# Quantising rows inside the product that follows, turned by transposing DMAs, and a ring of eight residual tiles in the last stage

## The chip, the cores and the metric

The kernel runs on one core of a Trainium2 chip. The metric is the device time in microseconds of one execution, the median of several runs. TensorE (PE) multiplies, ScalarE (ACT) evaluates functions, VectorE (DVE) and GpSimd (POOL) work elementwise, and SyncE (SP) and POOL issue the DMAs named below.

## The reference, cut to what matters

Two gated blocks, each attention and a feed-forward layer, run over x of 16 x 256 rows of 512 float32. The change touches the end of the second one only:

```python
h = _layernorm(x, ln_g, ln_b)
h = _qlinear(h, w1)                       # (4096 x 512) by (512 x 2048)
h = jax.nn.gelu(h, approximate=False)
out = _qlinear(h, w2)                     # (4096 x 2048) by (2048 x 512)
x = x + jnp.tanh(g_ffn[1]) * out

def _quant_act_int8(x):
    amax = jnp.maximum(jnp.quantile(jnp.abs(x), 1.0 - 0.005), EPS)
    s = 127 / amax
    q = jnp.clip(jnp.round(x * s), -128, 127) / s
```

`_qlinear` quantises its input by one scale for the whole tensor (`_quant_act_int8`) and its weights to -1, 0 and 1. The scale needs a quantile over all elements, so each of the two layers has to wait for a search.

## The kernel before, in words

The 4096 rows are 32 tiles of 128 rows (`TILES`), in 8 batches (`NB`) of 4 tiles (`WB`). The program is a row of stages. Each is a block with a list for each engine and semaphores of its own, and ends in two barriers of all engines with the clearing of the semaphores between them (L113 is the barrier), so work of one stage doesn't overlap that of the next. The stages that matter:

- `quantile1` (to L1833) finds `amax1`, the first scale, and puts the ternary first weights into `w1T`.
- `quantise_hidden` (L1836): for each of 8 batches DVE rounds (L1864) and clips (L1866) `hid`, 128 x 2048 float32, in place. ACT converts it to bf16 integers `q` (L1878), TensorE transposes its 16 blocks of 128x128 into PSUM (L1895), and ACT and DVE each copy a half to `qT` (L1881, L1869). An identity for TensorE is loaded by SP first (L1850), and DVE begins with a cast of it (L1856), then `full` and `scale` (L1857, L1859). TensorE runs a batch behind DVE and ACT.
- `product_tops` (L1919): 32 groups of products (L1904), 28 wide ones (2 tiles, half of the 2048 columns) and 4 narrow ones (1 tile, all columns). Two PSUM halves `bz` take turns. ACT applies gelu (L1961, L1959) into `Gs`, three buffers of four tiles: two lie in the memory of `hid`, which is free by then, the third is its own. SP spills each tile, 1 MB, to `g_d` (the tensor `activations`, L1934), and DVE takes maxima of every tile into `cand` (L1975). From the fourth batch on ACT waits until the batch that lay in its buffer is spilled and its maxima are taken.
- `quantile2` finds the second scale from `cand` and makes `w2T`.
- `ffn` (L2186), run once as `p8_`: SP reloads the spilled tiles (L2235) into 13 slots, the last three batches being resident. ACT counts (L2283) and rounds every second tile (L2285), DVE rounds the others (L2315), clips all into a ring of four `Gq` (L2320), TensorE multiplies (L2267), and DVE adds the residual (L2339). `output(n)` runs on DVE `LAG` = 3 tiles behind. The residual comes by POOL's queue in batches of 4 tiles, 1 MB, into two buffers `y` (L2246), and the sums are stored from them (L2252). A new batch can be loaded when the store of the one that lay in the buffer has landed. The last batch is stored by SP, tile by tile (L2238).
- `quantile2_of_all` and a second `ffn` (`p9_`) are run only if a flag says that the search over the maxima wasn't enough.

The order on each queue is the order of the code. `groups` and `ready` are tables written out before the run: group i belongs to tiles n, n + 1, and `ready[n]` is the number of gelus after which tile n is complete.

## Time and profile before

| | |
|---|---|
| time, median of 3 runs (lowest, highest) | 1515.62 us (1513.62, 1519.42) |
| the profiled execution | 1515.95 us |
| its span on the core | 1514.1 us |
| busy: PE, DVE, ACT, POOL | 1237.0, 996.2, 733.6, 352.3 us |
| bytes moved by DMA | 261.85 MB, 173 GB/s in the mean |

The rows that the prediction uses stand further below, in numbered groups. In a timeline each row has the start of an instruction or of a merged run of them in us from the start of the span, its length, the engine (SPq is a DMA issue on SP), the line, the operation with output and inputs, the count, and in brackets the idle time of the engine just before it, with what ended it. Buffer names are the program's, with the number left out and prefixes cut to p_ or q_; `residual` is the DRAM tensor that POOL loads `y` from. A stretch row gives busy time by engine and, behind it, the clock that TensorE was granted (1.00 is full) and the mean busy share of the 16 DMA engines.

### The profile page before, as it was taken

The page shows a single profiled execution, that of the slowest core. Times are in us where ns is not written, and L with a number is a line of the kernel's source. Part 1 is how long each engine was busy: PE and PEld are TensorE (multiplying, and loading weights), DVE is VectorE, ACT ScalarE, POOL GpSimd, SP SyncE. Part 2 cuts the span into 40 slices and gives each one's busy share as a digit, 9 for nine tenths or more (in the row PEclk, how much of TensorE's full clock was granted, in tenths as well). Part 3 has the DMA queues.
Part 4 walks back from the last instruction along what each step waited for, and adds up shares of the span by engine and source line. Part 5 has one row for each costly group of instructions (what it writes and reads, how often), then busy time and mean ns, then how long its engine had stood idle before and what let it go on. Part 6 is the DMA issues. An engine that isn't in the chain of part 4 may idle for free. (4 is left out here: it accounts for less than half of the span.)

```text
span 1514.1 us, 25958 instructions
## 1 busy us (share of the span) xinstructions
PE 1237.0 (82%) x9458; PEld 922.0 (61%) x9458; DVE 996.2 (66%) x2309; ACT 733.6 (48%) x1129; POOL 352.3 (23%) x339
## 2 busy tenths in 40 slices
PE   6899999999999846999993999992424999246986
PEld 5788888888888735766651566651313888242433
DVE  5677777767766633444432599994776699676573
ACT  3233333333343321456442466663835555677990
POOL 1233333333343230111000167663000000000120
PEclk9999999999999967999997999995555999556998
DMA  6032122221222119689668999933000577215973
GB/s 220 22 112 71 72 77 90 96 85 70 74 72 101 47 57 372 214 292 317 231 241 323 380 330 329 345 121 127 18 1 3 227 310 325 87 56 214 399 275 113
DMA packets 89723, 261.85 MB, mean 173 GB/s; under 512 B 9585, under 2 KB 21009, under 8 KB 81425
## 3 DMA queue, kind: packets, MB, share of 16 engines
q1 hardware_dynamic: 78976, 226.81, 40.1%
q0 software_dynamic: 7664, 32.51, 6.3%
q10 hardware_dynamic: 2976, 1.14, 0.3%
q8 instruction: 63, 1.03, 0.3%
q14 instruction: 44, 0.35, 0.1%
HBM read 155.32 MB, written 105.12 MB: 172 GB/s over the span
## 5 line engine op out<-in xcount | busy, mean ns | idle before, releaser
L921 PEld LDWEIGHTS p_sel<-p_pick,p_xp 128*128 128x128 bf16 x1536 | 89.3, 100 | 59.0 <-issue 34.1
L921 PE MATMUL p_sel<-p_pick,p_xp 128*128 128x128 bf16 x1536 | 100.6, 224 | 25.4 <-DMA p_xp<-xparts 22.4
L1904 PE MATMUL p_z<-qT,w1T 128*128 128x256 bf16 (+1 forms) x1152 | 113.9, 263 | 2.1 <-PEq L113 2.1
L1059 DVE COPY p_selT<-p_sel 128x512 f32<-128x512 f32 x64 | 44.3, 692 | 104.2 <-PE p_sel L921 104.2
L1904 PEld LDWEIGHTS p_z<-qT,w1T 128*128 128x128 bf16 x1152 | 102.6, 98 | 13.4 <-issue 2.4
L2246 POOL DMA_DIRECT2D p_y<-residual x8 | 8.4, 1053 | 392.6 <-POOLq L113 335.3
L2267 PE MATMUL p_o<-w2T,p_Gq 128*128 128x512 bf16 x384 | 88.4, 392 | 11.5 <-DVE p_Gq L2320 11.5
L1975 DVE MAX8 cand<-hid 128x8 f32<-128x128 f32 x384 | 75.1, 277 | 16.9 <-ACT hid L1961 16.9
L1004 ACT ACTIVATE p_selT<-p_sel 128x512 f32<-128x512 f32 x64 | 38.2, 597 | 91.1 <-PE p_sel L921 91.1
L341 PE MATMUL p_M<-p_ctxTh,p_Wkh 128*128 128x256 f32 x256 | 76.0, 297 | 1.9 <-DVE p_Wkl L667 1.9
L341 PE MATMUL p_M<-p_xnTh,p_Wqh 128*128 128x256 f32 x256 | 75.0, 293 | 0.8 <-DVE p_V L740 0.8
L2267 PEld LDWEIGHTS p_o<-w2T,p_Gq 128*128 128x128 bf16 x384 | 38.3, 101 | 60.5 <-DVE p_Gq L2320 13.0
L341 PE MATMUL p_M<-p_ctxTh,p_Wkl 128*128 128x256 f32 x256 | 73.1, 286 | 0.0
L341 PE MATMUL p_M<-p_ctxTl,p_Wkh 128*128 128x256 f32 x256 | 73.0, 285 | 0.0
L341 PE MATMUL p_M<-p_xnTh,p_Wql 128*128 128x256 f32 x256 | 72.1, 282 | 0.0
L341 PE MATMUL p_M<-p_xnTl,p_Wqh 128*128 128x256 f32 x256 | 72.0, 281 | 0.0
L511 ACT ACTIVATE p_qT<-p_M,p_bqT 128x256 f32<-128x256 f32 x64 | 26.8, 470 | 84.0 <-PE p_M L341 84.0
L1253 PE MATMUL p_O<-p_cin,p_eT 128*128 128x512 f32 x128 | 62.9, 619 | 2.2 <-ACT p_eT L1321 2.2
L1728 PE MATMUL q_tot<-q_cnt,q_ones 128*128 128x4 f32 x32 | 9.2, 359 | 65.4 <-DVE q_junk L1778 33.0
L1235 PE MATMUL p_S<-p_ctxT,p_xnT 128*128 128x256 f32 x256 | 61.1, 382 | 0.2 <-ACT p_xnT L1307 0.2
L962 PE MATMUL p_lay<-p_f,p_inner 64*128 64x512 f32 x208 | 58.5, 639 | 2.8 <-DVE p_stage L1051 2.8
L601 POOL TENSOR_TENSOR p_xb<-p_xin,p_tgbo 128x1024 f32<-128x1024 f32 x16 | 39.0, 2439 | 91.2 <-DVE p_sharedk L791 75.0
(320 smaller groups left out, 3519.1 us busy)
## 6 DMA issues: line engine op xcount, KB each, us to landing
inter_d<-p_stage SPq DMA_DIRECT2D x64, 512.0 KB, 4.3
p_rows<-inter_d SPq DMA_DIRECT2D x32, 1024.0 KB, 9.0
activations<-hid SPq DMA_DIRECT2D x24, 1024.0 KB, 6.0
p_cin<-in_ctx_dram SPq DMA_DIRECT2D x32, 512.0 KB, 5.2
xparts<-p_parts SPq DMA_DIRECT2D x16, 768.0 KB, 3.2
hid<-activations SPq DMA_DIRECT2D x10, 1024.0 KB, 10.2
p_xp<-xparts SPq DMA_DIRECT2D x3, 3072.0 KB, 25.1
p_xin<-in_x_dram SPq DMA_DIRECT2D x16, 512.0 KB, 4.1
```

Of the source, the lines that this page charges most:

```text
L341: mm = pe.matmul(out, left[a][:, c, lcols], right[e][:, c, rcols], start=(k == 0), stop=(k == len(terms) - 1))
L511: a = act.activation(dst[:, c, :], bM[k][:, (c % 2) * S:(c % 2 + 1) * S], ACT.Identity, bias=bias[:, c:c + 1])
L601: pool.tensor_tensor(xb[par][:, :, :], xin[par][:, :, :], tgbo[:, :].rearrange("p (a d) -> p a d", a=1).broadcast_to([P, NT, D]), ALU.add) ...
L921: mm = pe.matmul(bsel[u % 2][:, k * P:(k + 1) * P], xp[:, c, tile, r, :], pick[sb % 2][:, tile, :, :].rearrange("p s g -> p (s g)"), start ...
L962: mm = pe.matmul(bank(n, a)[:, :], inner[rows, j, h * P:(h + 1) * P], f2s[i // PAIRS][rows, j % (PAIRS // 2), :], start=True, stop=True)
L1004: act.activation(*picked(q, u), ACT.Copy).then_inc(s["sel_act"], 1)
L1059: dve.tensor_copy(*picked(q, u)).then_inc(s["sel_dve"], 1)
L1235: mm = pe.matmul(bS[:, t * S:(t + 1) * S], xnT[:, c, t * P:(t + 1) * P], ctxT[b % 2][:, c, :], start=(c == 0), stop=(c == C - 1))
L1253: mm = pe.matmul(bO[t][:, :], eT[:, k, t, :], cin[b % CD][:, k, :], start=(k == 0), stop=(k == NT - 1))
L1904: mm = pe.matmul(bank, w1T[:, c, fc * P:(fc + 1) * P], qT[:, c, bass.ds(first, n)], start=(c == 0), stop=(c == C - 1))
L1975: a = dve.max(cand[:, c:c + 8], Gs[j % R][:, t, :, k * OCT:(k + 1) * OCT])
L2267: mm = pe.matmul(bo[n % len(bo)][:, :], Gq[n % QR][:, k, :], w2T[:, k, :], start=(k == 0), stop=(k == FC - 1))
```

## The change

`quantise_hidden` goes. Its work moves into `product_tops`, in pairs of tiles (`NPAIR` = 16):

- DVE computes `full` and `scale`, then rounds and clips all 16 pairs of `hid` one after the other, with the product's own scale `zs` after the second; its maxima come behind them.
- ACT converts pairs 0 to 4 at once and the other eleven after the first eight gelus (2, 1, 1, 2, 1, 1, 2, 1 of them), into a ring of four bf16 buffers `q`.
- SP issues one transposing DMA for each pair (128 x 1024 bf16, 256 KB, on-chip memory to on-chip memory), nine before the first spill and the others among the spills. TensorE waits for the pair's DMA at each group.
- `qT` is now laid out by tile, [P, TILES, C, P], so a product over two tiles reads two runs of 128 columns. No identity, no transposes on TensorE, no copies out of PSUM. One stage with its barriers less.
- `Gs` changes its order: the buffer outside `hid` comes first, and ACT waits at the second and third batch until the pairs that lie there are converted.

In `ffn` the two `y` buffers of four tiles become eight of one tile (`YR`), each with its semaphores. POOL loads and stores tiles of 256 KB: a store after each tile, and behind it a load into the buffer whose store was issued `BEHIND` = 2 tiles before, once that has landed. `LAG` is 4.

```diff
-def quantise_hidden(nc, hid, K, amax, scale, qT):
...
 PAIR = 2 * P
 HALF = FC // 2
 NARROW = WB
+NPAIR = TILES // 2
+
+
+def z_product(pe, bank, w1T, qT, fc, first, tiles):
+
+    for c in range(C):
+        mm = pe.matmul(bank, w1T[:, c, fc * P:(fc + 1) * P], qT[:, bass.ds(first, tiles), c, :], start=(c == 0), stop=(c == C - 1))
+    return mm
 
 
...
 
-def product_tops(nc, qT, w1T, gam, amax, zs, Gs, g_d, cand):
+def product_tops(nc, hid, qT, w1T, gam, amax, zs, Gs, g_d, cand):
 
     groups = product_groups()
     ready = [max(i for i, (first, tiles, *_) in enumerate(groups) if first <= n < first + tiles) + 1 for n in range(NB * WB)]
+    QB, EARLY = 4, 5
+    late = list(range(EARLY, NPAIR))
+    after_gelu = {g: [late.pop(0) for _ in range(k)] for g, k in enumerate((2, 1, 1, 2, 1, 1, 2, 1))}
+    assert not late
     with ExitStack() as es:
         bz = [es.enter_context(nc.psum_tensor(f"p7_z{i}", [P, FC * P], F32)) for i in range(2)]
-        s = es.enter_context(semaphores(nc, "p7_", ["scale_own", "scale_done", "z_full", "gelu_done", "max_done"] + [f"spilled{i}" for i in range(len(Gs))]))
+        q = [es.enter_context(nc.sbuf_tensor(f"p7_q{i}", [P, 2, D], BF16)) for i in range(QB)]
+        full, scale = [es.enter_context(nc.sbuf_tensor("p7_" + n, [P, 1], F32)) for n in ("full", "scale")]
+        s = es.enter_context(semaphores(nc, "p7_", ["own", "scale_done", "rounded", "clipped", "q_done", "z_full", "gelu_done", "max_done"]
+                                        + [f"turned{i}" for i in range(QB)] + [f"spilled{i}" for i in range(len(Gs))]))
         block = es.enter_context(nc.Block())
         R = len(Gs)
+        pair = lambda k: hid[:, 2 * k:2 * k + 2, :]
 
         @block.sync
         def _(sp):
+
+            def turn(k):
+                sp.wait_ge(s["q_done"], k + 1)
+                sp.dma_start_transpose(qT[:, 2 * k:2 * k + 2, :, :].rearrange("p t c n -> p (t c) n"), q[k % QB][:, :, :].rearrange("p t d -> p (t d)")).then_inc(s[f"turned{k % QB}"], 16)
+
+            turns = 0
             for n in range(NB * WB):
+                while turns < min(NPAIR, 9 + 3 * (n // 2)):
+                    turn(turns)
+                    turns += 1
                 j, t = divmod(n, WB)
                 sp.wait_ge(s["gelu_done"], ready[n])
                 sp.dma_start(g_d[:, j, t], Gs[j % R][:, t]).then_inc(s[f"spilled{j % R}"], 16)
@@ -1938,15 +1891,26 @@
         @block.tensor
         def _(pe):
             for i, (n, tiles, f0, nf) in enumerate(groups):
+                k = n // 2
+                pe.wait_ge(s[f"turned{k % QB}"], 16 * (k // QB + 1))
                 if i >= 2:
                     pe.wait_ge(s["gelu_done"], i - 1)
                 bank = bz[i % 2][:, :].rearrange("p (f n) -> p f n", f=nf)
                 for f in range(nf):
-                    mm = z_product(pe, bank[:, f, :], w1T, qT, f0 + f, n * P, tiles * P)
+                    mm = z_product(pe, bank[:, f, :], w1T, qT, f0 + f, n, tiles)
                 mm.then_inc(s["z_full"], 1)
 
         @block.scalar
         def _(act):
+
+            def integers(k):
+                act.wait_ge(s["clipped"], k + 1)
+                if k >= QB:
+                    act.wait_ge(s[f"turned{k % QB}"], 16 * (k // QB))
+                act.activation(q[k % QB][:, :, :], pair(k), ACT.Copy, bias=-MAGIC).then_inc(s["q_done"], 1)
+
+            for k in range(EARLY):
+                integers(k)
             act.wait_ge(s["scale_done"], 1)
             for i, (n, tiles, f0, nf) in enumerate(groups):
                 j, t = divmod(n, WB)
@@ -1954,19 +1918,36 @@
                     if t == 0 and f0 == 0:
                         act.wait_ge(s[f"spilled{j % R}"], 16 * WB * (j // R))
                     act.wait_ge(s["max_done"], n - R * WB + tiles)
+                elif j and t == 0 and f0 == 0:
+                    act.wait_ge(s["q_done"], j * NPAIR // 2)
                 act.wait_ge(s["z_full"], i + 1)
                 if tiles == 1:
                     act.activation(Gs[j % R][:, t], bz[i % 2][:, :].rearrange("p (f n) -> p f n", f=nf), ACT.Gelu, scale=zs[:, 0:1]).then_inc(s["gelu_done"], 1)
                 else:
                     act.activation(Gs[j % R][:, t:t + tiles, f0:f0 + nf, :], bz[i % 2][:, :].rearrange("p (f t n) -> p t f n", f=nf, t=tiles),
                                    ACT.Gelu, scale=zs[:, 0:1]).then_inc(s["gelu_done"], 1)
+                for k in after_gelu.get(i, ()):
+                    integers(k)
 
         @block.vector
         def _(dve):
-
-            dve.tensor_scalar(zs[:, 0:1], amax[:, 0:1], 1.0 / QMAX, None, ALU.mult).then_inc(s["scale_own"], 1)
-            dve.wait_ge(s["scale_own"], 1)
-            dve.tensor_tensor(zs[:, 0:1], zs[:, 0:1], gam[:, 0:1], ALU.mult).then_inc(s["scale_done"], 1)
+            n_ = Count(dve)
+
+            def own():
+                dve.wait_ge(s["own"], n_.next(s["own"]))
+
+            dve.reciprocal(full[:, :], amax[:, 0:1]).then_inc(s["own"], 1)
+            own()
+            dve.tensor_scalar(scale[:, :], full[:, :], QMAX, None, ALU.mult).then_inc(s["own"], 1)
+            own()
+            for k in range(NPAIR):
+                dve.tensor_scalar(pair(k), pair(k), scale[:, :], MAGIC, ALU.mult, ALU.add).then_inc(s["rounded"], 1)
+                dve.wait_ge(s["rounded"], k + 1)
+                dve.tensor_scalar(pair(k), pair(k), MAGIC + QMAX, MAGIC + QMIN, ALU.min, ALU.max).then_inc(s["clipped"], 1)
+                if k == 1:
+                    dve.tensor_scalar(zs[:, 0:1], amax[:, 0:1], 1.0 / QMAX, None, ALU.mult).then_inc(s["own"], 1)
+                    own()
+                    dve.tensor_tensor(zs[:, 0:1], zs[:, 0:1], gam[:, 0:1], ALU.mult).then_inc(s["scale_done"], 1)
             for n in range(NB * WB):
                 j, t = divmod(n, WB)
                 dve.wait_ge(s["gelu_done"], ready[n])
...
-    R, QR, LAG = len(Gs), 4, 3
+    R, QR, LAG, YR, BEHIND = len(Gs), 4, 4, 8, 2
...
-        y = [sbt(f"y{i}", [P, WB, D]) for i in range(2)]
+        y = [sbt(f"y{i}", [P, D]) for i in range(YR)]
...
-                for t in range(WB):
-                    sp.wait_ge(s["y_done"], WB * (NB - 1) + t + 1)
-                    sp.dma_start(ov[:, order[NB - 1] * WB + t, :], y[(NB - 1) % 2][:, t, :]).then_inc(s["y_last"], 16)
+                for n in range(NB * WB - WB, NB * WB):
+                    sp.wait_ge(s["y_done"], n + 1)
+                    sp.dma_start(ov[:, token_tile(n), :], y[n % YR][:, :]).then_inc(s["y_last"], 16)
                 sp.wait_ge(s["y_last"], 16 * WB)
 
         @block.gpsimd
         def _(pool):
             with when(pool, flag):
 
-                def load_x(i):
-                    pool.dma_start(y[i % 2][:, :, :], x3_d[:, order[i] * WB:(order[i] + 1) * WB, :]).then_inc(s[f"x_in{i % 2}"], 16)
-
-                load_x(0)
-                load_x(1)
-                for i in range(NB - 1):
-                    pool.wait_ge(s["y_done"], WB * (i + 1))
-                    pool.dma_start(ov[:, order[i] * WB:(order[i] + 1) * WB, :], y[i % 2][:, :, :]).then_inc(s[f"y_out{i % 2}"], 16)
-                    if i + 2 < NB:
-                        pool.wait_ge(s[f"y_out{i % 2}"], 16 * (i // 2 + 1))
-                        load_x(i + 2)
-                for par in range(2):
-                    pool.wait_ge(s[f"y_out{par}"], 16 * len(range(par, NB - 1, 2)))
+                def load_x(n):
+                    pool.dma_start(y[n % YR][:, :], x3_d[:, token_tile(n), :]).then_inc(s[f"x_in{n % YR}"], 16)
+
+                for n in range(YR):
+                    load_x(n)
+                for n in range(NB * WB - WB):
+                    pool.wait_ge(s["y_done"], n + 1)
+                    pool.dma_start(ov[:, token_tile(n), :], y[n % YR][:, :]).then_inc(s[f"y_out{n % YR}"], 16)
+                    m = n - BEHIND
+                    if m >= 0 and m + YR < NB * WB:
+                        pool.wait_ge(s[f"y_out{m % YR}"], 16 * (m // YR + 1))
+                        load_x(m + YR)
+                for k in range(YR):
+                    pool.wait_ge(s[f"y_out{k}"], 16 * len(range(k, NB * WB - WB, YR)))
 
...
                 def output(n):
-                    i, t = divmod(n, WB)
+                    here = y[n % YR][:, :]
                     dve.wait_ge(s["o_used"], n + 1)
-                    if t == 0:
-                        dve.wait_ge(s[f"x_in{i % 2}"], 16 * (i // 2 + 1))
-                    dve.scalar_tensor_tensor(y[i % 2][:, t, :], bo[n % len(bo)][:, :], coef[:, :], y[i % 2][:, t, :], ALU.mult, ALU.add).then_inc(s["y_done"], 1)
+                    dve.wait_ge(s[f"x_in{n % YR}"], 16 * (n // YR + 1))
+                    dve.scalar_tensor_tensor(here, bo[n % len(bo)][:, :], coef[:, :], here, ALU.mult, ALU.add).then_inc(s["y_done"], 1)
 
...
-    Gs = [room[:, k * FC:(k + 1) * FC, :].rearrange("p (t a) (b n) -> p t (a b) n", t=WB, b=WB) for k in range(2)] + [sbt("third", [P, WB, FC, P])]
+    Gs = [sbt("third", [P, WB, FC, P])] + [room[:, k * FC:(k + 1) * FC, :].rearrange("p (t a) (b n) -> p t (a b) n", t=WB, b=WB) for k in range(2)]
...
-        qT = sbt("qT", [P, C, TILES * P], BF16)
-        quantise_hidden(nc, hid, K, amax1, scale, qT)
+        qT = sbt("qT", [P, TILES, C, P], BF16)
```

## Rows read from the trace of the kernel before

**Rows 1.** The page: the span, and the queue of the small constants.

```profile
span 1514.1 us, 25958 instructions
...
q10 hardware_dynamic: 2976, 1.14, 0.3%
```

**Rows 2.** Stretches: length, busy us (count) of PE, PEld, DVE, ACT, POOL, clock, DMA share, GB/s.

```profile
1131.00:1171.40 40.40, 14.69 (x128) 12.63 (x129) 25.48 (x28) 22.69 (x16) 0.00 (x0) 0.54 0.01 3
...
1182.00:1291.70 109.70, 103.28 (x1072) 93.88 (x1069) 100.22 (x512) 59.10 (x31) 0.00 (x0) 0.99 0.75 307
...
1412.00:1424.00 12.00, 12.00 (x57) 5.49 (x56) 3.69 (x4) 11.81 (x11) 2.03 (x2) 1.00 1.01 422
```

**Rows 3.** Timeline (start, us, engine): the quantising stage and the product's start.

```profile
1136.13 0.33 SPq L1850 DMA_DIRECT2D p_ident<-in_c_ident_dram  x1
1137.98 0.23 DVE L1856 CAST p_identb<-p_ident 128x128 bf16<-128x128 f32 x1 [6.86 <-DMA p_ident<-in_c_ident_dram]
...
1138.51 1.29 DVE L1864 TENSOR_SCALAR hid<-hid,scale 128x2048 f32<-128x2048 f32 x1
...
1140.97 1.28 DVE L1864 TENSOR_SCALAR hid<-hid,scale 128x2048 f32<-128x2048 f32 x1
...
1167.39 1.89 PE L1895 MATMUL p_t<-p_identb,p_q 128*128 128x128 bf16 x16 [1.53 <-ACT p_q L1878]
...
1171.42 11.79 PE L1904 MATMUL p_z<-qT,w1T 128*128 128x256 bf16 x92 [2.14 <-PEq L113]
```

**Rows 4.** Timeline of ACT and DVE in the product, beginning and end.

```profile
1176.67 1.28 ACT L1961 ACT_TABLE_LOAD   x1 [6.33 <-PE p_z L1904]
...
1182.11 6.28 DVE L1975 MAX8 cand<-hid 128x8 f32<-128x128 f32 x32 [10.34 <-ACT hid L1961]
...
1183.69 1.97 ACT L1961 ACTIVATE hid<-p_z,zs 128x2048 f32<-128x2048 f32 x1 [1.61 <-PE p_z L1904]
1187.18 1.97 ACT L1961 ACTIVATE hid<-p_z,zs 128x2048 f32<-128x2048 f32 x1 [1.53 <-PE p_z L1904]
...
1285.37 1.97 ACT L1959 ACTIVATE hid<-p_z,zs 128x2048 f32<-128x2048 f32 x1 [1.61 <-PE p_z L1904]
```

**Rows 5.** Timeline of ACT and DVE in the search before: operations on 128x1024.

```profile
1119.34 1.06 ACT L1712 ACTIVATE q_junk_a<-q_over 128x1024 bf16<-128x1024 f32 x1
...
1124.14 0.75 DVE L1765 TENSOR_SCALAR q_junk<-cand,q_cur 128x1024 f32<-128x1024 f32 x1
```

**Rows 6.** DMA issues: out<-in, queue, count, KB each, median us to landing.

```profile
p_vrep<-global_values SPq DMA_DIRECT2D x16, 256.0 KB, 3.5
...
out_dram<-p_y SPq DMA_DIRECT2D x4, 256.0 KB, 2.0
```

**Rows 7.** Timeline of PE in the last stage.

```profile
1380.55 13.29 PE L2267 MATMUL p_o<-w2T,p_Gq 128*128 128x512 bf16 x48 [6.04 <-DVE p_Gq L2320]
...
1397.13 10.52 PE L2267 MATMUL p_o<-w2T,p_Gq 128*128 128x512 bf16 x48
1407.49 3.62 PE L2267 MATMUL p_o<-w2T,perm 128*128 128x512 bf16 x16
...
1425.36 10.53 PE L2267 MATMUL p_o<-w2T,p_Gq 128*128 128x512 bf16 x48 [0.45 <-DVE p_Gq L2320]
...
1440.77 10.53 PE L2267 MATMUL p_o<-w2T,p_Gq 128*128 128x512 bf16 x48 [1.42 <-DVE p_Gq L2320]
...
1458.30 11.97 PE L2267 MATMUL p_o<-w2T,p_Gq 128*128 128x512 bf16 x48 [3.55 <-DVE p_Gq L2320]
```

**Rows 8.** Timeline of DVE in the last stage: one of three waits for the residual.

```profile
1423.42 0.75 DVE L2339 SCALAR_TENSOR_TENSOR p_y<-p_o,p_coef,p_y 128x512 f32<-128x512 f32 x1 [8.18 <-DMA p_y<-residual]
```

**Rows 9.** Timeline of POOL in the last stage.

```profile
1413.52 0.58 POOL L2246 DMA_DIRECT2D p_y<-residual  x1 [11.42 <-DMA out_dram<-p_y]
1414.09 1.45 POOL L2252 DMA_DIRECT2D out_dram<-p_y  x1
1428.68 0.53 POOL L2246 DMA_DIRECT2D p_y<-residual  x1 [13.14 <-DMA out_dram<-p_y]
```

69 lines of the change are left out of this document (5 added, 64 removed).

## The prediction

> **What bounds the kernel now.** I read the stretches first, then the timelines of the three stages that the diff touches, then the DMA rows. The profiled execution took 1515.95 us, of which 1514.1 are its span [rows 1]; the rest lies around the span and I leave it as it is. The median of the three runs is 1515.62, so 0.3 less than the profiled one.
>
> The stages stand one behind the other, with barriers between them, so each is worth what its own chain is worth. The quantising stage is a stretch in which no engine is full: in 40.4 us DVE is busy 25.5, ACT 22.7, TensorE 14.7, and the DMA engines hardly at all [rows 2]. TensorE's 128 transposes there only serve the layout. The product behind it is bound by TensorE: it starts at 1171.42 [rows 3], and from then on ACT's gelus come 3.49 us apart (1187.18 after 1183.69), the 32nd at 1285.37; DVE's maxima of a pair of tiles take 6.28 of each 6.99 us and wait for ACT in the rest [rows 4]. In the last stage TensorE needs 3.45 us a tile (1407.49 - 1397.13 for three), but stands idle three times, 0.45, 1.42 and 3.55 us, for a quantised tile that DVE has not made [rows 7]. DVE in turn was held by the load of the residual, 8.18 us at 1423.42 [rows 8].
>
> **Part 1, the start of the product.** I work out when TensorE can start in the changed kernel.
> - The block starts where the old one did. SP issues the first DMA of the old block at 1136.13; DVE waited for it until 1137.98 [rows 3]. The new DVE waits for nothing, so reciprocal and scale start near 1136.2. In the trace the cast, the reciprocal and the scale take 1138.51 - 1137.98 = 0.53, without the cast about 0.4: first rounding at 1136.6.
> - A pair of tiles is 128x1024. Such a DVE operation takes 0.75 us [rows 5]; the clip behind it is taken the same less the overlap, 0.7. Pair 0 is clipped at 1138.1. The following pairs come 1.4 us apart, by half of 1140.97 - 1138.51 = 2.46, the pitch of four tiles (DVE's second rounding stands at 1140.97), and a little for a fixed cost that doesn't halve. All 16 pairs are done near 1136.6 + 16 x 1.4 + 0.4 = 1159.4.
> - ACT's conversion of 128x1024 to bf16: 1.06 us [rows 5], done at 1139.1.
> - The transposing DMA of that pair, 256 KB. The trace has none. The nearest rows by size are 2.0 us (SP, 256 KB, contiguous pieces of 2 KB, idle engines) and 3.5 us (256 KB) from issue to landing [rows 6]. By the code each of 128 partitions receives 8 runs of 128 bf16, which is 1024 pieces of 256 B. Queue 10, with 2976 packets of 383 B on average in 0.3% of 16 engines' span [rows 1], gives 0.003 x 16 x 1514 / 2976 = 24 ns a piece, so 1024 x 24 / 16 = 1.6 us on the engines. If the pieces are smaller: 3.1 us at 128 B, 6.2 at 64 B, 12.5 at 32 B. I take 1.6 on the engines and 3.9 from issue to landing, because 256 B is what the destination's layout gives; the ends are 2.0 and 12.5 + 2.0.
> - TensorE starts at 1139.1 + 3.9 = 1143.0 instead of 1171.42: **28.4 us** earlier.
> - It starts colder. The first group ended 5.25 us after its start (1176.67 - 1171.42), 1.8 over the pitch, after transposes at a granted clock of 0.54 on average [rows 2 to 4]. The last stage's first 48 products, after 6.04 us of idling, took 13.29 against 10.52, 2.8 over [rows 7]. New idle time is 12 us, so I take 2.8: **1.0 us** is given back. The barrier and the semaphore clearing of the stage that goes lie within the 28.4 already.
>
> Once started, what can hold TensorE back? A pair lasts 7.0 us there. DVE delivers one each 1.4 us. ACT has 3.49 - 1.97 = 1.5 us free beside a gelu; the 11 late conversions cost 1.06 each and fall into eight gaps, at most two in one, 0.6 over in three of them, repaid in the next since two banks lie between; the first of them is needed 35 us later. I cost them at nothing. Should ACT reload its table at each change between gelu and copy, eight round trips of 2 x 1.28 [rows 4] would cost up to 20 us; the trace has one load before the first gelu only, and the search behind it mixes gelu and sign without any. DVE is 1159.4 - 1154.7 = 4.7 us late with its first maxima (1182.11 moved 27.4 earlier is 1154.7), and makes up 0.71 a pair, so it is level after 7 of 14 pairs, before the tail. TensorE reads qT in two runs of 128 columns instead of one of 256; no row shows a price for that, and I take 0, at most one fortieth of the stage, 3 us. The 16 pairs' q buffers are a ring of four, read out by the DMA long before.
>
> **Part 2, SP's queue.** SP now issues 9 turns before the first spill, then up to 3 before each two. A wait for a conversion there holds back all the spills queued behind it: turn 8 waits for the conversion behind the third gelu, near 1157. The gelu of tile 16 writes over tiles 4 to 7, so it waits for spill 7, behind all 16 turns and 8 MB of spills. One MB takes 2.5 us at 422 GB/s [rows 2]. With E the time of one turn on the engines, spill 7 lands no sooner than 1139.1 + 16 E + 20 + 2. ACT wants it at 1143.0 + 5.25 + 16 x 3.49 = 1204.1. So the turns cost nothing up to **E = 2.7 us**, and 16 us for each us beyond. My 1.6 is below. On the whole the DMA engines had a quarter of the stage free (share 0.75 [rows 2]), 27 us, which holds 16 x 1.6.
>
> **Part 3, the residual in a ring.** Before, a 1 MB load could only be issued when the 1 MB store of its buffer had landed: load at 1413.52, next store at 1414.09, its landing releases the load at 1428.68 [rows 9]. In the ring a load waits for one 256 KB store made two tiles ago, and lies six tiles = 20.7 us ahead of its use. While the engines are full (share 1.01 [rows 2]) POOL's queue moved 2 MB in 1428.68 - 1413.52 = 15.2 us, 138 GB/s; the ring asks for 0.5 MB in 3.45 us, 152 GB/s. It falls behind by 0.35 us a tile at most, over some 16 tiles 5.6 us, which the 20.7 cover. So the three idle times go, 5.42 us, and with them the slow restart after the longest, 11.97 - 10.53 = 1.44 [rows 7]: 6.9 us. LAG 4 lets the output find its product done; TensorE sets the pace either way, so 0. POOL issues 60 DMAs instead of 15; those of before took 0.53 to 1.45 us [rows 9], so two a tile, a load and a store, about 2.0 and at most 2.9 of 3.45. That is close, and I take **6.4 us**; the ends are 0 and 6.9 (and 1 us loss, if the ring holds TensorE once more than before).
> The Trainium skill (SBUF — State Buffer, "SBUF: two separate sides") says that a DVE operation in a two-port mode locks GpSimd out, so that it can't write descriptors. That speaks against 60 small DMAs. Here POOL's issues beside such DVE work are the 0.53 to 1.45 us used above; by the page they would stretch further and the gain of this part would go to 0.
>
> **Sum.** 28.4 - 1.0 + 6.4 = 33.8. 1515.95 - 33.8 = 1482.1; less 0.3 for the median, **1482 us**. Beyond that I expect no other stage to move.
>
> **Rivals.**
> 1. *The turns fill the DMA engines* (E over 2.7). Place: SP's ring, spill 7 before tile 16. For it: no row shows a transposing DMA, and one whose pieces are below 256 B costs 3.1 to 12.5 us by the packet rate. Against it: the destination has runs of 256 B. (a) E = 3.1: 6.6 us lost, 1489 us. (b) It ends slower than before where 16 (E - 2.7) exceeds 33.8, from **E = 4.8**. At E = 6.2: 1161.1 + 99.2 - 1204.1 = 56 us lost, 1538 us.
> The Trainium skill (VectorE: DVE Perf Modes, "The three transpose paths") gives 1309 ns for 128x128 bf16 by DMA and 390 ns by TensorE. A pair is 8 such blocks; if they don't overlap, E is an estimated 10.5 us and the time an estimated 1482 + 125 = 1607. Another page (Advanced Engine Details and Errata, "X-Bar Transpose (TRN2)") expects 350 to 400 GB/s, an estimated 0.7 us a pair. No row here decides between them.
> 2. *The ring gives nothing.* POOL, queued behind its wait for an old store, issues the next store late, and loads of 2 KB pieces get a smaller share beside loads of 8 KB. TensorE is idle as before: 1482 + 6.4 = 1488 us.
> 3. *The merge doesn't overlap.* Something that I count as covered (ACT's table, a slow first turn of 10 us, strided reads of qT) takes 5 to 20 us: 1487 to 1502.
>
> **Chances.** Forecast 0.57; rival 2 0.12; rival 1a, E from 2.7 to 4.8, 0.12; rival 1b 0.14; rival 3 0.05. A measurement can tell about 0.5%, 7.6 us, from no change. Faster than 1508: 0.57 + 0.12 + 0.05 + 0.09 of 1a = 0.83. Within: 0.02 of 1a. Slower than 1523: 0.15, nearly all 1b. The range goes down to 1477 (a first turn of 2.0 us, no colder start, the full 6.9, and a little), and up over rivals 2, 3 and most of 1a to 1508; 0.17 is left out, most of it 1b.
>
> **What the changed profile would show.** The first matmul of the product near 1143, with the first turn landing just before. Turns of under 2.7 us pitch on the engines, and no idle time of TensorE between the first group and the last; gelus 3.49 us apart. DVE's quantising of 16 pairs in 22.8 us in one block, and its maxima level with ACT by mid-stage. In the last stage no wait of DVE for the residual beyond 3 tiles' cushion, 32 tiles in 110.6 + 2.8 us. Wrong would be the prediction if ACT waited for spills from tile 12 or 16 on (rival 1), if POOL's issues filled its time (rival 2), or if the first group came only after 1150 (rival 3).

## The result, and the profile after

The changed kernel took **1478.97 us** (median of four runs, 1477.86 to 1480.85), the kernel before 1516.5 beside it (four runs, 1513.62 to 1519.42): a ratio of 0.975, interval 0.9733 to 0.9767. The forecast was 1482, the range 1477 to 1508. In the profiled executions it is 1480.85 against 1515.95, so 35.1 us less where the sum said 33.8. By the medians it is 37.5 us here, and 33.7 and 33.5 in the two further groups of runs below (1481.68 against 1515.38, 1481.05 against 1514.51): the forecast lies inside that scatter.

The page of the changed kernel: span, busy time by engine, and the queues with packets, MB and their share of the 16 DMA engines.

```profile
span 1479.1 us, 25797 instructions
PE 1222.5 (83%) x9330; PEld 909.8 (62%) x9330; DVE 986.6 (67%) x2316; ACT 726.5 (49%) x1129; POOL 384.5 (26%) x384
q1 hardware_dynamic: 95728, 230.95, 42.8%
```

To find where the time went, I measured both traces from a common mark, the operation that makes `amax`, which both run alike. The start of a search is its first DMA issue, the closing sum is the product of `p_total` behind the last tile. The mark in the kernel before and in the changed one:

```profile
1130.97 0.15 DVE L1652 TENSOR_SCALAR amax<-amax 128x1 f32<-128x1 f32 x1
1130.98 0.15 DVE L1652 TENSOR_SCALAR amax<-amax 128x1 f32<-128x1 f32 x1
```

| us after the mark | before | after | gained up to here |
|---|---|---|---|
| the product's first matmul | 40.45 | 11.64 | 28.8 |
| start of the search behind it | 161.78 | 133.97 | 27.8 |
| the last stage's first matmul | 249.58 | 221.63 | 27.95 |
| the last stage's closing sum | 371.32 | 336.17 | 35.15 |

So the merge brings 28.8 us and gives 1.0 back within the stage, and the last stage brings 7.2. Between them nothing moves by more than 0.2. These distances are a finer measure than whole times: the code ahead of the mark is the same in all fourteen traces, yet the mark lies anywhere from 1127.56 to 1134.41 us, while the closing sum of the changed kernel came 336.17, 336.34 and 335.33 us behind it in its three traces. Differences below 1 us between traces are within that scatter.

**The merged stage**, timeline of the changed kernel (start, duration, engine, line, operation; in brackets the idle time before it and what ended it; a merged row's duration includes the waits between its instructions):

```profile
1136.57 0.75 DVE L1944 TENSOR_SCALAR hid<-hid,p_scale 128x1024 f32<-128x1024 f32 x1
1137.36 0.69 DVE L1946 TENSOR_SCALAR hid<-hid 128x1024 f32<-128x1024 f32 x1
1137.97 0.75 DVE L1944 TENSOR_SCALAR hid<-hid,p_scale 128x1024 f32<-128x1024 f32 x1
1138.09 1.06 ACT L1910 ACTIVATE p_q<-hid 128x1024 bf16<-128x1024 f32 x1 [17.58 <-DVE hid L1946]
1139.17 21.31 SPq L1878 DMA_TRANSPOSE qT<-p_q  x9
1142.62 7.61 PE L1845 MATMUL p_z<-qT,w1T 128*128 128x256 bf16 x49 [12.12 <-DMA qT<-p_q]
...
1148.46 1.28 ACT L1927 ACT_TABLE_LOAD   x1 [3.49 <-PE p_z L1845]
1149.75 1.97 ACT L1927 ACTIVATE third<-p_z,zs 128x2048 f32<-128x2048 f32 x1
1151.62 1.99 ACT L1910 ACTIVATE p_q<-hid 128x1024 bf16<-128x1024 f32 x2
1153.52 1.96 ACT L1927 ACTIVATE third<-p_z,zs 128x2048 f32<-128x2048 f32 x1
...
1159.09 7.04 DVE L1956 MAX8 cand<-third 128x8 f32<-128x128 f32 x36
...
1257.50 1.97 ACT L1925 ACTIVATE hid<-p_z,zs 128x2048 f32<-128x2048 f32 x1 [1.60 <-PE p_z L1845]
```

Every step of the forecast's start has its row: first rounding 1136.57, pair 0 clipped at 1138.05 (1137.36 + 0.69), a pair each 1.40 us (1137.97 - 1136.57), conversion 1138.09 to 1139.15, turn issued at 1139.17, first matmul 1142.62. The table is loaded once, before the first gelu, though eleven copies follow between gelus. The last gelu starts at 1257.50 (before: 1285.37, [rows 4]).

TensorE stands still once behind its start, for 0.3 us near 1155.5. The first two groups are ready before the first gelu ends, so in the kernel before ACT went from gelu to gelu there with 0.18 us between:

```profile
1180.11 1.97 ACT L1961 ACTIVATE hid<-p_z,zs 128x2048 f32<-128x2048 f32 x1 [0.18 <-PE p_z L1904]
```

In the changed kernel two conversions stand in that place, and the second gelu ends at 1155.48 (1153.52 + 1.96); the fourth group needs its bank. From the first gelu to the fourth it is 9.56 us instead of 9.22 (1159.31 - 1149.75 against 1187.18 - 1177.96). The other nine late conversions cost nothing more.

What the turns did, the answer for the tile `qT` (duration on SP's queue in ns, min/median/max; then the landing, counted from the issue):

```profile
L1878 SPq DMA_TRANSPOSE qT<-p_q x16: 1232/1319/4288, 1139.2 to 1181.6; - x16
DMA to landing us min/median/max: 3.0/3.4/8.9
```

On the page of before the same queue reads:

```profile
q1 hardware_dynamic: 78976, 226.81, 40.1%
```

So it has 16752 packets and 4.14 MB more now. 16 turns of 262144 bytes are 4.19 MB, less 0.07 MB for the identity that is no longer loaded; in pieces of 256 bytes they are 16384 packets. Both fit, the packets to 368.

The nine turns ahead of the first spill hold SP for 1.23 to 1.88 us and land after 3.0 to 4.0. The seven between the spills hold it for 1.31 to 4.29 us and land after 3.2 to 8.9; in convert first and no overlap (below), where all sixteen lie ahead of the spills, none held SP for more than 1.38 us or landed later than 4.4.

Stretches of the changed kernel: length, busy us (count) of PE, PEld, DVE, ACT, POOL, granted clock, DMA share, GB/s.

```profile
1143.00:1160.00 17.00, 16.90 (x137) 13.92 (x135) 16.59 (x29) 13.08 (x11) 0.00 (x0) 0.88 0.51 96
1160.00:1264.00 104.00, 97.40 (x1018) 88.63 (x1015) 98.81 (x508) 62.78 (x36) 0.00 (x0) 0.98 0.94 344
1365.00:1425.00 60.00, 60.00 (x279) 27.18 (x278) 47.29 (x48) 59.25 (x50) 23.48 (x29) 1.00 1.02 418
```

While the turns run with no spill beside them, the DMA engines are half full; behind it, with the spills, nearly full.

**The last stage**, TensorE's timeline, then the waits of DVE and POOL there (total us, times, longest), and the two DMA lines of POOL:

```profile
1352.61 13.46 PE L2250 MATMUL p_o<-w2T,p_Gq 128*128 128x512 bf16 x48 [6.05 <-DVE p_Gq L2303]
1365.90 3.62 PE L2250 MATMUL p_o<-w2T,perm 128*128 128x512 bf16 x16
1369.36 10.52 PE L2250 MATMUL p_o<-w2T,p_Gq 128*128 128x512 bf16 x48
...
1462.60 3.62 PE L2250 MATMUL p_o<-w2T,perm 128*128 128x512 bf16 x16
```
```profile
DVE p_y L2321 <- DMA p_y<-residual: 2.5, 3, 1.4
...
POOL p_y L2228 <- DMA out_dram<-p_y: 32.5, 15, 3.8
POOL out_dram L2234 <- DVE p_y L2321: 23.7, 10, 9.3
```
```profile
L2228 POOL DMA_DIRECT2D p_y<-residual x32: 546/933/1567, 1349.8 to 1448.4; - x32
DMA to landing us min/median/max: 3.3/8.4/13.7
...
L2234 POOL DMA_DIRECT2D out_dram<-p_y x28: 539/539/1269, 1366.7 to 1454.7; - x28
DMA to landing us min/median/max: 2.3/6.8/12.3
```

The three idle times of [rows 7] are gone; the matmuls stand behind one another from 1352.61 on. DVE's three waits for the residual were 21.2 us before (8.18 of them in [rows 8]) and are 2.5 now, at most 1.4 each, and TensorE never feels them. POOL still waits 32.5 us for stores, but in fifteen short pieces.

### The profile page after: what moved, and what is told of

It reads as the page before. It is cut to its first block and busy times, and to the rows that moved or that the text cites. A ratio compares the mean times of both kernels' runs of the same rounds, so it can differ in the third digit from the quotient of the medians.

```text
span 1479.1 us, 25797 instructions
## 1 busy us (share of the span) xinstructions
PE 1222.5 (83%) x9330; PEld 909.8 (62%) x9330; DVE 986.6 (67%) x2316; ACT 726.5 (49%) x1129; POOL 384.5 (26%) x384
## 3 DMA queue, kind: packets, MB, share of 16 engines
q8 instruction: 62, 1.02, 0.3%
## 5 line engine op out<-in xcount | busy, mean ns | idle before, releaser
L2228 POOL DMA_DIRECT2D p_y<-residual x32 | 29.5, 924 | 340.3 <-POOLq L113 307.4
L1956 DVE MAX8 cand<-hid 128x8 f32<-128x128 f32 x320 | 62.3, 273 | 2.8 <-ACT hid L1927 2.8
L591 POOL TENSOR_TENSOR p_rs<-p_ve,p_mhalf 128x2 f32<-128x2 f32 x32 | 22.3, 698 | 151.1 <-DVE p_ve L657 151.0
```

The source lines that it names most:

```text
L1956: a = dve.max(cand[:, c:c + 8], Gs[j % R][:, t, :, k * OCT:(k + 1) * OCT])
L2228: pool.dma_start(y[n % YR][:, :], x3_d[:, token_tile(n), :]).then_inc(s[f"x_in{n % YR}"], 16)
```

## The experiments

Kernels whose ratios are compared ran on one chip, beside runs of the kernel before: first group (part 1 alone, part 2 alone, the changed kernel again, warm), second (turns twice, turns in halves, no overlap, convert first), third (the changed kernel a third time, turns twice and earlier, ring of four, LAG 3). Diffs are against the changed kernel unless said otherwise.

**Part 1 alone**: the changed kernel with the last stage of before.

```
-R, QR, LAG, YR, BEHIND = len(Gs), 4, 4, 8, 2
+R, QR, LAG = len(Gs), 4, 3
...
-y = [sbt(f"y{i}", [P, D]) for i in range(YR)]
+y = [sbt(f"y{i}", [P, WB, D]) for i in range(2)]
...
```

The loads, stores and the output are those of before too.

> The changed kernel with the last stage of before (two residual buffers of four tiles, LAG 3). Theory: the two parts are independent, because barriers lie between the stages. Then TensorE's first product stays at 1142.6, the search behind the product starts 27.8 us sooner than before as in the changed kernel, and the time is 37.5 - 7.3, so about 30 us or at least 28 us, below before: ratio 0.980 to 0.982. The three idle times of TensorE in the last stage, 5.4 us, are back. Rival: the parts interact (the later spills leave DMA work that slows the last stage): a ratio of 0.984 or more.

Measured 1485.64 us (1484.21 to 1488.21), ratio 0.980, interval 0.9777 to 0.9822. TensorE's idle times are back, and DVE's waits with them (timeline of PE in the last stage, and DVE's waits there):

```profile
1398.50 10.53 PE L2248 MATMUL p_o<-w2T,p_Gq 128*128 128x512 bf16 x48 [0.60 <-DVE p_Gq L2301]
...
1430.74 12.22 PE L2248 MATMUL p_o<-w2T,p_Gq 128*128 128x512 bf16 x48 [4.44 <-DVE p_Gq L2301]
```
```profile
DVE p_y L2320 <- DMA p_y<-residual: 20.8, 3, 10.9
```

0.60 + 4.44 + (12.22 - 10.53) = 6.7 us, and the trace is 6.9 longer than the changed kernel's over both marks (343.09 - 336.17).

**Part 2 alone**: the kernel before with the ring and LAG 4 of the changed one.

```
-R, QR, LAG = len(Gs), 4, 3
+R, QR, LAG, YR, BEHIND = len(Gs), 4, 4, 8, 2
...
-y = [sbt(f"y{i}", [P, WB, D]) for i in range(2)]
+y = [sbt(f"y{i}", [P, D]) for i in range(YR)]
...
```

The loads, stores and the output are those of the change too.

> The kernel before with the eight-tile residual ring and LAG 4 alone. Theory: TensorE has no idle time between the first and last product of the last stage, 7 us shorter than before: ratio 0.995 to 0.996. Rival (the ring gives nothing, POOL held by its waits): ratio 0.999 to 1.001 and idle times of TensorE as before.

Measured 1509.63 us (eight runs, 1507.22 to 1511.48), ratio 0.9956, interval 0.9939 to 0.9972: against 1515.38 for the kernel before that is 5.8 us in the runs and 7.5 in the trace (371.32 - 363.85). TensorE has no idle time there. Together the parts add up: 28.2 (371.32 - 343.09) + 7.5 = 35.7, and the whole change is 35.15, the same within the scatter of the traces. So neither part lives off the other, and the interval leaves out 1: the ring alone is worth some 0.4%.

**The changed kernel again, and warm.** Warm adds products whose result nothing reads, into a bank that is free, ahead of the first product of either stage. They are extra work, nothing is left out.

```
         def _(pe):
+            for _ in range(18):
+                pe.matmul(bz[1][:, 0:512], w1T[:, 0, 0:P], w1T[:, 0, 0:512], start=True, stop=True)
...
             with when(pe, flag):
+                for _ in range(7):
+                    pe.matmul(bo[-1][:, :], w2T[:, 0, 0:P], w2T[:, 0, :], start=True, stop=True)
```

> The changed kernel again, so that the three others are compared with it on the same chip: ratio 0.975 as before, within 0.002.

> The changed kernel, and TensorE computes 18 products of 128x512 whose results are thrown away before the first product of the merged stage, and 7 before the first of the last stage. Theory: the first group costs 5.84 us instead of 3.49 and the first 48 products of the last stage 13.46 instead of 10.52 because the granted clock is at its lower level after idling; busy beforehand, both start at the higher one. That gives up to 2.3 + 2.9 = 5.2 us: about 1474 against 1479. Rival: the slow first group is not the clock but the first reads or the releases, or the clock doesn't rise on thrown-away products: no change, 1479. If the 7 products are too few, only 2.3 us or less come.

Measured: again 1481.68 us (1477.61 to 1483.63), ratio 0.9771, interval 0.9747 to 0.9796; warm 1479.01 (1472.89 to 1479.24), ratio 0.9747, interval 0.9721 to 0.9772. Between the kernels' marks warm is 4.2 us shorter (336.34 - 332.13), and 3.2 against the shortest of the changed kernel's three traces (335.33). Its timeline and stretches:

```profile
1137.74 6.11 PE L1894 MATMUL p_z<-w1T 128*128 128x512 bf16 x18 [5.90 <-PEq L113]
1144.17 5.09 PE L1845 MATMUL p_z<-qT,w1T 128*128 128x256 bf16 x45 [0.32 <-DMA qT<-p_q]
1147.92 1.28 ACT L1929 ACT_TABLE_LOAD   x1 [1.40 <-PE p_z L1845]
```
```profile
1137.70:1144.20 6.50, 6.14 (x19) 2.22 (x20) 6.22 (x13) 3.30 (x4) 0.00 (x0) 0.67 0.34 65
1144.20:1148.00 3.80, 3.80 (x36) 3.41 (x36) 3.70 (x6) 2.06 (x3) 0.00 (x0) 1.00 0.93 178
```

and, for comparison, the same place in the changed kernel:

```profile
1131.00:1142.60 11.60, 0.00 (x0) 0.00 (x0) 6.31 (x14) 3.25 (x4) 0.00 (x0) 0.50 0.20 38
1142.60:1148.00 5.40, 5.38 (x31) 3.96 (x32) 5.26 (x9) 2.04 (x2) 0.00 (x0) 0.60 0.87 167
```

After 11.6 us without a matmul the granted clock stands at 0.50, the lower of TensorE's two levels (1.2 GHz); with products thrown away before it, it is 1.00 (2.4 GHz) from the first useful one on. The first group then takes 3.75 us (1147.92 - 1144.17) instead of 5.84 (1148.46 - 1142.62), 2.1 less. The same group took 5.22 to 6.11 us in all the other traces of the changed kernel and its variants that start with it after idling, so this is clear of scatter, and here the mechanism is shown.

In the last stage it is less clear. The first 48 products take 11.34 us instead of 13.46, again 2.1, but the clock was at 0.50 all through the seven thrown-away ones, 0.60 in the two microseconds behind them, and only then 1.00. In the thirteen traces without them the same 48 took anywhere from 11.51 to 13.48 us. So that the seven products brought the 2.1 isn't shown. In the times the two intervals overlap: that this version beats the changed kernel is likely, but not shown.

**No overlap**: all sixteen pairs are converted and turned before the first product; the stage of its own is gone, the turning is by DMA, but nothing runs beside TensorE's product that didn't before.

```
-QB, EARLY = 4, 5
+QB, EARLY = 4, NPAIR
...
-after_gelu = {g: [late.pop(0) for _ in range(k)] for g, k in enumerate((2, 1, 1, 2, 1, 1, 2, 1))}
+after_gelu = {g: [late.pop(0) for _ in range(k)] for g, k in enumerate(())}
...
-while turns < min(NPAIR, 9 + 3 * (n // 2)):
+while turns < min(NPAIR, NPAIR):
...
+for k in range(NPAIR - QB, NPAIR):
+    pe.wait_ge(s[f"turned{k % QB}"], 16 * (k // QB + 1))
 for i, (n, tiles, f0, nf) in enumerate(groups):
```

> The changed kernel, but all 16 pairs are converted and turned before TensorE's first product: the turns by DMA stay, the merging is undone. Theory (the gain is the overlap alone, turning by DMA is slower than TensorE's transposes): 16 turns at SP's 2.5 us end at 1139 + 40 + 1 = 1180, the product starts 38 us later than in the changed kernel and 9 later than before, about 1517, so 1 to 2 us over the kernel before in spite of the ring. Rival (turns at DVE's pace, 1.4 us a pair): first product at 1164, about 1500.

Measured 1503.41 us (1500.91 to 1503.89), ratio 0.9924, interval 0.99 to 0.9949. The rival's number held, mine didn't: the first matmul comes 32.72 us after the mark, against 40.45 before and 11.64 in the changed kernel. Of the 28.8 us, 7.7 come from turning in another way, without TensorE's transposes, their evictions and the barrier, and 21.1 from the overlap. The run also measures the turn: timeline, then the stretch in which nothing but turns is on the DMA engines.

```profile
1138.53 22.38 SPq L1878 DMA_TRANSPOSE qT<-p_q  x16
...
1163.06 1.22 PE L1845 MATMUL p_z<-qT,w1T 128*128 128x256 bf16 x5 [33.21 <-DMA qT<-p_q]
```
```profile
1145.00:1150.00 5.00, 0.00 (x0) 0.00 (x0) 4.86 (x8) 3.89 (x4) 0.00 (x0) 0.50 0.98 186
```

The engines are just full, a share of 0.98 at 186 GB/s here and 1.01 at 191 in the five microseconds behind, so a turn costs them 262144 B / 189 GB/s = 1.4 us, the very pitch at which DVE delivers pairs. The Trainium skill (VectorE: DVE Perf Modes, "The three transpose paths") gives 1309 ns for a 128x128 block. The 10.5 us that I estimated from it for the eight blocks of a pair don't hold: eight blocks in one DMA cost 1.4 us. Whether one block alone takes 1309 ns no run here shows. The Trainium skill (Advanced Engine Details and Errata, "X-Bar Transpose (TRN2)") expects 350 to 400 GB/s, about twice what runs here.

**Convert first**: the same EARLY and turns, without the wait in front of the first product. ACT converts all sixteen pairs before its first gelu.

```
-QB, EARLY = 4, 5
+QB, EARLY = 4, NPAIR
...
-while turns < min(NPAIR, 9 + 3 * (n // 2)):
+while turns < min(NPAIR, NPAIR):
```

> The changed kernel, but ACT converts all 16 pairs before its first gelu, and SP issues all turns before the first spill. The ring of four bf16 buffers ties each conversion to the turn four before it. Theory (SP's 2.5 us a turn paces them): the last conversion ends near 1139 + 11 x 2.5 + 3.5 + 1 = 1171, so the first gelu comes there instead of 1148.5 and TensorE stands idle after two groups for 22 us: about 1501. Rival (conversions run at DVE's 1.4 us): first gelu at 1162, about 1492.

Measured 1493.31 us (two runs, 1493.26 and 1493.36), ratio 0.9859, interval 0.9829 to 0.989. The rival held again: it takes DVE's pace of 1.4 us a pair, not ACT's 1.06.

```profile
1161.99 3.83 ACT L1927 ACTIVATE third<-p_z,zs 128x2048 f32<-128x2048 f32 x2
1164.10 16.13 PE L1845 MATMUL p_z<-qT,w1T 128*128 128x256 bf16 x130 [11.85 <-ACT third L1927]
```

TensorE stands 11.85 us at its third group, for the gelu that frees the bank of the first. So the late conversions, woven between the gelus, are what makes an early start worth having: without them 13.4 of the 21.1 us are lost (147.32 - 133.97).

**Turns twice**: each turn is issued a second time into scratch, and PE and ACT wait for both. What the DMA engines and SP's queue spend on turning doubles.

```
 sp.dma_start_transpose(qT[:, 2 * k:2 * k + 2, :, :].rearrange("p t c n -> p (t c) n"), q[k % QB][:, :, :].rearrange("p t d -> p (t d)")).then_inc(s[f"turned{k % QB}"], 16)
+sp.dma_start_transpose(spare_T[k % QB][:, :, :, :].rearrange("p t c n -> p (t c) n"), q[k % QB][:, :, :].rearrange("p t d -> p (t d)")).then_inc(s[f"turned{k % QB}"], 16)
...
-pe.wait_ge(s[f"turned{k % QB}"], 16 * (k // QB + 1))
+pe.wait_ge(s[f"turned{k % QB}"], 32 * (k // QB + 1))
...
-act.wait_ge(s[f"turned{k % QB}"], 16 * (k // QB))
+act.wait_ge(s[f"turned{k % QB}"], 32 * (k // QB))
```

> The changed kernel, but SP issues every turn twice, the second time into a scratch tensor of its own, and TensorE and ACT wait for both. In the profile of the changed kernel SP issued 9 turns in 21.3 us and later 3 in 7.5, 2.5 us each, while the 16 DMA engines' share was 0.51. Theory A (the engines set the price, 1.2 to 1.6 us a turn): with two, 2.4 to 3.2 us a pair, TensorE starts 2.5 us later and nothing else waits: about 1482. Theory B (SP is held 2.5 us by each turn, and the spills queue behind it): 5 us a pair, the twelfth pair's turn ends near 1199 and the sixteenth near 1219, the gelus of tiles 12 and 16 wait for spills: some 25 us more, about 1504.

Measured 1489.21 us (1488.84 to 1491.72), ratio 0.9838, interval 0.9812 to 0.9863: between the theories. The start is 1.35 us later (12.99 against 11.64), and TensorE stands once more, in the middle of the stage:

```profile
1177.53 1.06 ACT L1912 ACTIVATE p_q<-hid 128x1024 bf16<-128x1024 f32 x1 [4.20 <-DMA p_w<-p_q]
...
1182.69 3.53 PE L1845 MATMUL p_z<-qT,w1T 128*128 128x256 bf16 x19 [4.38 <-ACT hid L1929]
```
```profile
1145.00:1160.00 15.00, 14.90 (x122) 12.42 (x121) 14.62 (x23) 10.88 (x9) 0.00 (x0) 0.91 1.02 173
```

ACT works in order. Its conversion waited 4.20 us for a turn that lay behind two 1 MB spills in SP's queue (the turn issued right behind them, at 1167.53, landed after 9.0 us; the median is 3.5), because the ring of `p_q` has four buffers; the gelu behind it was late by that much, and TensorE by 4.38. The engines are full at 173 GB/s, 1.5 us a turn. That is another place than the one I had named (the gelu of tile 16, waiting for spill 7).

**Turns twice, and earlier**: as above, but twelve turns ahead of the first spill and four more for each two.

```
-while turns < min(NPAIR, 9 + 3 * (n // 2)):
+while turns < min(NPAIR, 12 + 4 * (n // 2)):
```

> The kernel with each turn issued twice, but SP issues 12 turns before the first spill and 4 more before each two, instead of 9 and 3. In the profile of the first, ACT's conversions stood 4.2 and 1.0 us for a turn that lay behind two spills in SP's queue (9 us to landing instead of 3.3), gelus and TensorE behind them, 4.4 us. Theory (the place in the queue costs, not the price of a turn): that wait goes, and the time falls by 4 to 5 us from 1489 to about 1485. Rival (the spills now come too late, spill 3 is what the gelu of tile 12 waits for): the stall only moves, 1489 or more.

Measured 1489.85 us (1488.1 to 1492.72), ratio 0.9834, interval 0.9805 to 0.9864. The rival held: the stall moved and the time stayed. ACT no longer waits for turns; the gelu of tile 12 waits for the spills of the buffer it writes over:

```profile
1198.74 3.82 ACT L1929 ACTIVATE third<-p_z,zs 128x2048 f32<-128x2048 f32 x2 [7.79 <-DMA activations<-third]
1200.85 3.36 PE L1845 MATMUL p_z<-qT,w1T 128*128 128x256 bf16 x15 [4.92 <-ACT third L1929]
```

So at doubled load, about 2.8 to 3.0 us a pair, these two orders in SP's queue decide who waits, and the time is the same. That the load of the DMA engines sets it is likely, but only argued: 32 turns at 1.5 us are an estimated 48 us of DMA work, where the product before had some 27 us free [rows 2], and 7 to 9 us were lost.

**Turns in halves**: 32 turns of 128 KB instead of 16 of 256 KB, the same bytes; PE and ACT wait for both halves.

```
-sp.dma_start_transpose(qT[:, 2 * k:2 * k + 2, :, :].rearrange("p t c n -> p (t c) n"), q[k % QB][:, :, :].rearrange("p t d -> p (t d)")).then_inc(s[f"turned{k % QB}"], 16)
+for t in range(2):
+    sp.dma_start_transpose(qT[:, 2 * k + t, :, :], q[k % QB][:, t, :]).then_inc(s[f"turned{k % QB}"], 16)
...
```

> The changed kernel with each turn split into two of one tile, 128 KB each. Same bytes, twice the instructions. If SP's 2.5 us a turn goes with the bytes (or pieces), a half takes 1.25 and the time stays at 1479 within 2 us. If it is a price of the instruction, a pair costs 5 us on SP and the time goes to about 1504, as in the kernel with each turn issued twice.

Measured 1482.26 us (1479.08 to 1483.3), ratio 0.9779, interval 0.9753 to 0.9806; in the trace the search starts 1.6 us later than in the changed kernel (135.53 - 133.97). The turns of this kernel:

```profile
L1879 SPq DMA_TRANSPOSE qT<-p_q x32: 1188/1267/2838, 1140.6 to 1193.6; - x32
...
DMA to landing us min/median/max: 2.4/2.5/8.2
```

SP is held 1.27 us by half a turn and 1.32 by a whole one: it pays by the instruction, the engines by the byte (all medians). Half a turn lands after 2.5 us, a whole one after 3.4. The turns of nine pairs now take SP 25.03 us instead of 21.31, and that is felt at the ring of four `p_q` buffers again: ACT waits once for a turn, and the gelu behind it comes 6.12 us after the one before instead of 3.76.

```profile
1175.60 2.00 ACT L1911 ACTIVATE p_q<-hid 128x1024 bf16<-128x1024 f32 x2 [2.25 <-DMA qT<-p_q]
```

That is most of the 1.6 us of the trace; in the times it doesn't stand out.

**A ring of four**: the residual in four buffers of one tile, each load behind the store of the tile before; two sizes change at once, the depth and how far back the store lies.

```
-R, QR, LAG, YR, BEHIND = len(Gs), 4, 4, 8, 2
+R, QR, LAG, YR, BEHIND = len(Gs), 4, 4, 4, 0
```

> The changed kernel with four residual buffers of one tile instead of eight (each reloaded as soon as the store just issued has landed). It tells the small tiles apart from the depth. Theory (the depth covers the slow transfers beside the reloads, 6.8 us a store and 8.4 a load in the median): a round trip of 15 us for each buffer against 4 x 3.45 = 13.8, and POOL waits for each store, 7 us a tile against 3.45, while the DMA engines are full, over some 16 tiles: TensorE is held up by 30 us or more, 1510 or more. Rival (tiles of 256 KB are enough, the depth is spare): 1479 to 1482.

Measured **1545.24 us** (1541.22 to 1548.35), ratio 1.0202, interval 1.0166 to 1.0238: 64 us over the changed kernel, and slower than the kernel before. Waits in the last stage:

```profile
POOL p_y L2228 <- DMA out_dram<-p_y: 105.9, 28, 6.7
DVE p_y L2321 <- DMA p_y<-residual: 84.9, 28, 6.9
```

Against the changed kernel's trace of this group the closing sum comes 59.7 us later behind the mark (395.01 - 335.33); TensorE waits 15.2 us for it behind the last tile, where it was 0.9. The mark itself lies 3.75 us later (1133.49 - 1129.74), where the code is the same, so some 60 of the 64 are the ring's. Each reloaded tile pays a whole round, store to landing and load to landing, 28 times. The direction is as I had written; I had worked out 30 us or more. It isn't the small DMAs that bring the gain, but the tiles of lead. How much of the 64 us is depth and how much the nearer store was not separated.

**LAG 3, beside the changed kernel a third time.**

```
-R, QR, LAG, YR, BEHIND = len(Gs), 4, 4, 8, 2
+R, QR, LAG, YR, BEHIND = len(Gs), 4, 3, 8, 2
```

> The changed kernel once more, on the chip of these three: ratio 0.976 within 0.002, so that the others are told apart from it and not only from the kernel before.

> The changed kernel with DVE's outputs 3 tiles behind instead of 4, the ring of eight kept. Theory (TensorE sets the pace, DVE's slack covers it): no change, 1479 to 1481, and no idle time of TensorE. Rival (with 3, DVE is held by the product before it makes the next integers): up to 1 us on each tile, 1485 or more.

Measured: LAG 3 1480.31 us (1475.82 to 1483.92), ratio 0.9777, interval 0.9744 to 0.981; the changed kernel 1481.05 (1479.06 to 1482.86), 0.9778, interval 0.9751 to 0.9805. No difference, and no idle time of TensorE in either. The LAG of the change is worth nothing by itself.

## Why the prediction was right, point by point

- **Start of TensorE** (forecast 28.4 earlier, measured 28.8). Landing was 3.4 us, not 3.9, and the first matmul came at 1142.62, not 1143.0. The price of a turn, the most uncertain term, came from the packet rate of another queue [rows 1]: 24 ns a piece gave 1.6 us on the engines, the runs show 1.4 to 1.5. There is luck in that: the queue's share is printed as 0.3%, so by rounding alone the price could have been 1.3 to 1.8 us, and that packets of a plain DMA cost what those of a turning one do was assumed. The piece of 256 bytes, read off the destination's layout, is confirmed by the packet count.
- **Colder start** (forecast 1.0 given back, measured 1.0 between the marks). The size is luck, because the division was wrong: the colder clock accounts for 0.6 of it (first group 5.84 us, before 5.25 [rows 3, 4]). From the first matmul to the last gelu it is 114.88 us (1257.50 - 1142.62), before 113.95 (1285.37 - 1171.42), so another 0.3 lies between the gelus, where I had put nothing. It is the first of the late conversions' gaps. And the 0.6 isn't fixed: in the other two traces of the changed kernel the first group took 5.92 and 5.29 us.
- **Late conversions at nothing, no table reload**: the table is loaded once, as forecast. The conversions cost 0.3 us, in one place: I had counted 1.5 us of ACT free beside each gelu, but between the first gelu and the second it has 0.2, and I had set two conversions there. What that delayed was not repaid in the next gap. Convert first shows what the cover is worth: 13.4 us.
- **DVE late and level by mid-stage**: held. The maxima start at 1159.09 (forecast 1159.4), and after seven pairs, from 1203.29 on, DVE waits for ACT again, 0.71 us a pair.
- **Strided reads of `qT` at nothing**: held. In no overlap, where no conversion lies between gelus and `qT` is read the same way, it is 107.49 us from the first gelu to the last, before 107.41, in the changed kernel 107.75 in each of its three traces. So the strides cost 0.1 us at most, and the rest is the conversions'.
- **SP's queue**: that the turns cost nothing held, and that the engines had room. The threshold E = 2.7 us did not hold: at 2.8 to 3.0 us a pair my line gives 16 x 0.3 = 5 us at most, the two runs lost 7 (140.94 - 133.97 at the search, turns twice, 1.35 of it at the start) and 8.8 (1489.85 - 1481.05 on one chip), and at other places. The step that failed is "the gelu of tile 16 waits for spill 7": it named one meeting point and took it for the first. A turn behind two spills meets the ring of four `p_q` buffers earlier, and the gelu of tile 12 meets spills 0 to 3. What I expected of turns twice rested also on a misreading of SP: the row of nine turns in 21.31 us includes SP's waits for ACT's conversions; the turn itself holds SP 1.32 us in the median (up to 4.29 between spills).
- **The ring** (forecast 6.4, ends 0 and 6.9; measured 7.2 in the whole change, 7.5 alone in the trace). The three idle times and the slow restart went. The rows' 6.9 was a little too small, because idle time is counted from the end of the last matmul, while two groups of products overlap by 0.17 us where nothing is between them (3.62 long, 3.45 apart). From start to start the three stops cost more [rows 7]. Four tiles without a stop take 13.81 us (4/3 of 1407.49 - 1397.13); the eight up to 1425.36 took 0.61 more than that, the four up to 1440.77 1.60 and the four up to 1458.30 3.72. With the restart's 1.44 that is 7.4 us; less the 0.17 by which the first 48 products were slower this time, that is the 7.2. POOL's issues took 0.54 to 1.57 us as the rows said; POOL was busy 23.48 of 60 us, and TensorE never stood. By my estimate the lock that the Trainium skill describes (SBUF — State Buffer, "SBUF: two separate sides") would have taken the gain to 0; the gain came in full. Whether DVE's operations here take that lock, and whether POOL's issues of up to 1.57 us are longer for it, no run shows.
- **The sum**: 33.8 forecast, 35.1 measured in the profiled executions. Of the 1.3 missing, 0.4 lie in the landing of the turn and 0.8 in the ring. That is no more than the scatter: 37.5, 33.7 and 33.5 by the medians of the three groups.
- **Rivals**: 1b, with its turn of 4.8 us or more, fell with the measured 1.4. Rival 2 is excluded by both part 1 alone and part 2 alone. Rival 3's number, 1487 to 1502, is about what the kernel costs where its overlap is taken away, by part or whole (1493.31, 1503.41); that the overlap would fail was what didn't happen.

## What to carry to other kernels

A stage that only serves the layout is worth its whole length less the first piece's latency, if the next stage can begin with a piece and each engine weaves the rest between its own work; here 21 of 29 us were this overlap and under 8 the cheaper way of turning. The price of a transposing DMA could be estimated before one was seen, by its pieces (the run of the destination) times the packet time of a queue with packets of like size (383 bytes here; queue 1's, of 2.9 KB, took 0.401 x 16 x 1514 us / 78976 = 123 ns each and would have given 7.9 us). It should also be checked for whom it stands in front of in its queue: look for every ring that the queue closes, not for one. A ring pays by the tiles of lead it gives over store plus load to landing under full DMA engines, and costs more than big buffers where it gives less. And a gap between two operations of an engine should be read at the very place where work is put into it: the first gap here had 0.2 us, the later ones 1.5.

## What the runs showed of the hardware that I had not expected

- A transposing DMA within SBUF in pieces of 256 bytes runs at 186 to 191 GB/s with the engines full, less than half of what plain 256 KB and 1 MB transfers reached in the last stage (418 GB/s at a share of 1.02). It holds SP 1.27 to 1.32 us in the median, whether it moves 128 or 256 KB, but up to 4.29 us when it is issued between spills.
- A turn behind two 1 MB spills in the same queue lands after up to 9.0 us (turns twice; 8.9 in the changed kernel) instead of 3.4, though the data never leaves SBUF.
- 256 KB loads and stores under full DMA engines took 8.4 and 6.8 us to land (median) in the ring of eight. In the ring of four, which keeps fewer in flight, the loads took 3.7; the DMA share was 0.81 from 1365 to 1425 us and 0.50 from 1425 to 1490, and the kernel was still some 60 us slower: with the engines half free, what is paid is the round of each tile, not the rate.
- Eighteen products thrown away before the start brought the granted clock from 0.50 to 1.00 by the first useful one, and cost no time at the start, as TensorE had nothing else to do: it came 11.84 us after the mark, in the changed kernel and in part 1 alone after 11.60 to 11.83.
